# A four-layer MetaFormer block: the first hidden unit and the router of each expert layer fed per image pair, two more casts on GpSimd, routing weights in two fp16 parts

## The reference, cut to what matters

```python
t = t + ffn(_ln_t(t), ...)                     # layer norm over the 64 channels of each pixel
# layer 1 (top 2 logits, softmax over these two); E = 8 experts, H = 256
gate_logits = xf @ Wg + bg
top_w, top_i = top_k(gate_logits, 2); top_w = softmax(top_w)
for e in range(8):
    h = gelu(xf @ W1[e] + b1[e])               # exact gelu
    out = out + w_dense[:, e:e+1] * (h @ W2[e] + b2[e])
# layers 2 and 3: H = 128, probs = softmax(all 8 logits), the two largest are kept as they are
# layer 0: H = 128, one routing per image: logits = mean over pixels @ Wr + br, softmax,
#          scaled by a capacity, softmax again, top 2, softmax; then a second layer norm
```

## Time and profile before

| | |
|---|---|
| median of three runs | 204.16 us |
| the profiled execution's own time | 204.11 us |
| its span, first to last instruction | 202.3 us |
| TensorE busy | 189.9 us (94%) |
| ScalarE / VectorE / GpSimd busy | 124.9 / 122.9 / 42.6 us |
| share of TensorE in the chain that ended last | 75%, VectorE 12%, ScalarE 5% |
| gelu on 128x1024 (L770), 40 of them | 44.4 us |
| down matmuls (L413) | 41.4 us |
| matmuls on zeros (L295), 99 of them | 27.0 us |

### The profile page before, as it was taken

How to read it: one execution, slowest core, us unless ns; L and a number is a source line. 1 busy time by engine, 2 the same in 40 slices (tenths; PEclk the granted TensorE clock), 3 DMA queues, 4 the chain that set the end, 5 groups by cost and what they waited for, 6 DMA issues and landing times.

```text
span 202.3 us, 3039 instructions
## 1 busy us (share of the span) xinstructions
PE 189.9 (94%) x1105; PEld 90.4 (45%) x1113; DVE 122.9 (61%) x342; ACT 124.9 (62%) x206; POOL 42.6 (21%) x60
## 2 busy tenths in 40 slices
PE   7999799889999999899999999999999998699994
PEld 2564222246977866423222346533225496242321
DVE  1358678995750543682824534487575688668565
ACT  2443888646245571876577570497786684588773
POOL 7851100000000000200995000020750022020570
DMA  6999500000000000000000000000000000000001
GB/s 206 369 410 404 209 3 2 0 0 3 0 5 0 0 0 3 0 3 2 0 0 0 0 3 0 0 0 0 0 5 2 0 0 5 0 0 0 0 3 52
DMA packets 3087, 8.54 MB, mean 42 GB/s; under 512 B 520, under 2 KB 1040, under 8 KB 2944
## 3 DMA queue, kind: packets, MB, share of 16 engines
q1 hardware_dynamic: 2736, 7.73, 10.1%
q0 software_dynamic: 192, 0.48, 0.7%
q10 hardware_dynamic: 144, 0.13, 0.3%
HBM read 8.08 MB, written 0.26 MB: 41 GB/s over the span
## 4 chain that ended last, share of the span: by engine, by line
PE 75%; DVE 12%; ACT 5%; issue 3%; POOL 2%; POOLq 1%; DVEq 0%; ACTq 0%
PE bank L413 16%; PE banks L364 8%; PE banks L295 7%; PE banks L365 6%; PE banks L590 6%; PE bank L306 4%; PE banks L348 4%; PE bank L300 3%; POOL total L1452 2%; PE banks L538 2%; PE bank L375 2%; PE bank L660 2%; PE bank L520 2%; ACT hidden L770 2%; PE banks L551 1%
## 5 line engine op out<-in xcount | busy, mean ns | idle before, releaser
L770 ACT ACTIVATE hidden<-banks,pack_l 128x1024 f32<-128x1024 f32 x40 | 44.4, 1113 | 17.0 <-PE banks L365 16.9
L413 PE MATMUL bank<-hidden,w 128*64 128x512 f32 (+1 forms) x160 | 41.4, 596 | 1.5 <-ACT hidden L770 1.5
L295 PE MATMUL banks<-idle_work 128*128 128x512 bf16 x99 | 27.0, 407 | 2.0 <-DVE idle_work L1053 1.2
L364 PE MATMUL banks<-split_x,w_hi 128*128 128x512 f16 x64 | 24.6, 384 | 0.0
L365 PE MATMUL banks<-split_x,w_lo 128*128 128x512 f16 x64 | 24.3, 379 | 0.0
L1443 POOL CAST split_x<-normed 64x256 f16<-64x256 f32 x8 | 3.9, 494 | 96.2 <-DVE normed L935 91.9
L733 ACT ACTIVATE squares<-bank 128x256 f32<-128x256 f32 x18 | 6.9, 383 | 24.1 <-PE bank L300 22.8
L1452 POOL TENSOR_TENSOR total<-total,term 128x512 f32<-128x512 f32 x12 | 17.1, 1424 | 1.9 <-DVE term L1030 1.3
L295 PEld LDWEIGHTS banks<-idle_work 128*128 128x128 bf16 x106 | 10.4, 103 | 14.5 <-issue 4.8
L364 PEld LDWEIGHTS banks<-split_x,w_hi 128*128 128x128 f16 x64 | 6.2, 97 | 23.2 <-issue 14.2
L413 PEld LDWEIGHTS bank<-hidden,w 128*64 128x64 f32 x160 | 7.9, 134 | 18.8 <-issue 16.5
(11 more groups left out here) (310 smaller groups left out, 322.6 us busy)
## 6 DMA issues: line engine op xcount, KB each, us to landing
w_stage<-in_w SPq DMA_DIRECT2D x3, 512.0 KB, 13.6
w_stage<-in_w SPq DMA_DIRECT2D x1, 1024.0 KB, 9.6
conv<-in_conv SPq DMA_DIRECT2D x1, 800.0 KB, 8.1
w<-in_w SPq DMA_DIRECT2D x3, 256.0 KB, 13.8
w<-in_w SPq DMA_DIRECT2D x1, 512.0 KB, 10.4
toeplitz<-in_toeplitz SPq DMA_DIRECT2D x1, 512.0 KB, 11.2
gauss<-in_gauss SPq DMA_DIRECT2D x1, 512.0 KB, 12.7
pack_l<-in_pack_l SPq DMA_DIRECT2D x1, 469.0 KB, 11.9
```

Of the source, the lines that this page charges most:

```text
L295: mm(out, idle_work[:, 0:128], idle_work[:, 0:cols], start=True, stop=True)
L364: mm(out, w1_hi[l][:, at:at + 128], split_x[h][:, :], start=True, stop=False)
L413: last = mm(out[64 * h:64 * h + 64, cut], w2[l][:, (f * NE + e) * CH:(f * NE + e + 1) * CH], hidden[v % 3][:, h * 512 + cut.start:h * 512 ...
L770: act(hidden[u % 3][:, :], both[u % 2][:, :], ACT.Gelu, bias=P(f"l{l}", "e_b1")[:, e * fc + f:e * fc + f + 1]).then_inc(S["moe_gelu"], 1)
```

## The change

It touches four things.

1. **TensorE's order at the start of an expert stage.** `up_straight` takes one chunk at a time (256 columns rather than 512) and waits only for that chunk of `normed`. In layers 1 to 3 the router does tiles 0 and 1 behind the first chunk and tiles 2 and 3 behind the second. In layer 1 the first chunk of unit 1 is also ahead of the second chunk of unit 0. `NORM_TAIL` falls from 4 to 2, 0, 1 and 1 ahead of the four expert stages.
2. **Casts.** ScalarE rounds only chunk 0 of half 0. GpSimd does three: chunk 0 of half 1, chunk 1 of half 1, chunk 1 of half 0. VectorE's last remainder waits for GpSimd's third cast.
3. **Smaller orders.** In layer 1 ScalarE finishes chunk 0's norm ahead of chunk 1's. In layer 0 VectorE takes over the scaling of the router weights, makes the remainders of chunk 0 ahead of the logits, and ScalarE's first exponential stands behind gelu(0).
4. **Routing weights.** The weight is multiplied by 1024 in the step that makes it; one cast writes its fp16 rounding to two places, one subtraction writes the remainder to two places; `select` holds 1/1024. `parts` and `rows` are 128 wide instead of 112, `spread` contracts 32 rows instead of 48.

```diff
-        parts = sb("parts", [128, TILES * 112], BF16)
-        rows = sb("rows", [112, COLS], BF16)
+        parts = sb("parts", [128, TILES * 128], F16)
+        rows = sb("rows", [128, COLS], F16)
...
-        NORM_TAIL = [5, 4, 4, 4, 4, 4, 4, 4, 4]
+        NORM_TAIL = [5, 2, 4, 4, 0, 4, 1, 4, 1]
...
-                    pe.wait_ge(S[f"l{l}_loaded"], 16)
-                    for i in range(TILES):
+                    pe.wait_ge(S["ln_rstd"], 2 * k + 2)
+                    for i in tiles:
                         last = mm(bank[7][:, i * 16:(i + 1) * 16], tile(normed[k], i), P(f"l{l}", "router"),
                                   start=True, stop=True)
-                    last.then_inc(S["route_logits"], 1)
+                    if i == TILES - 1:
+                        last.then_inc(S["route_logits"], 1)
...
-                        pe.wait_ge(S["ln_out"], 2 * k + 2)
+                        pe.wait_ge(S["ln_out"], 2 * k + j + 1)
                     for h in range(HALVES):
                         r = slice(64 * h, 64 * h + 64)
-                        last = mm(both[u % 2][:, h * 512:(h + 1) * 512], stage[l][r, at:at + 128], normed[k][r, :],
-                                  start=True, stop=True)
-                    last.then_inc(S["moe_hidden"], 1)
+                        last = mm(both[u % 2][:, h * 512 + j * PIX:h * 512 + (j + 1) * PIX], stage[l][r, at:at + 128],
+                                  chunk(normed[k], j)[r, :], start=True, stop=True)
+                    if j == INNER - 1:
+                        last.then_inc(S["moe_hidden"], 1)
...
                 for u in range(units):
-                    (up_straight if u < STRAIGHT else up_split)(u)
-                    if u == 0:
-                        router()
-                    if u == 1:
+                    if u == 0 and l == 0:
+                        up_straight(0, 0)
+                        up_straight(0, 1)
+                        router(())
+                    elif u == 0:
+                        up_straight(0, 0)
+                        router((0, 1))
+                        if l == 1:
+                            up_straight(1, 0)
+                        up_straight(0, 1)
+                        router((2, 3))
+                    elif u == 1:
+                        if l != 1:
+                            up_straight(1, 0)
+                        up_straight(1, 1)
                         pe.wait_ge(S[f"w2_loaded{l}"], 16)
+                    else:
+                        up_split(u)
...
-                for j in range(INNER):
-                    sc.wait_ge(S["ln_out"], 2 * k + j + 1)
-                    act(chunk(split_x[0], j)[0:64, :], chunk(normed[k], j)[0:64, :], ACT.Copy)\
-                        .then_inc(S["split_hi0"], 1)
+                sc.wait_ge(S["ln_out"], 2 * k + 1)
+                act(chunk(split_x[0], 0)[0:64, :], chunk(normed[k], 0)[0:64, :], ACT.Copy).then_inc(S["split_act"], 1)
                 nc.scalar.preload_act_table_set("gelu_and_others")
...
-                st.link(TT(g8(rt["weight"][:, :]), g8(rt["picked"][:, :]), spread_to(rs_["inv"][:, :], 8), ALU.mult))
...
-                st.link(V.tensor_copy(part[0], g28("weight")))
-                st.link(TT(g28("rem"), g28("weight"), part[0], ALU.subtract))
-                st.link(V.tensor_copy(part[1], g28("rem")))
-                st.link(TT(part[2], g28("rem"), part[1], ALU.subtract))
-                V.tensor_copy(by_tile[:, :, 64:112], by_tile[:, :, 0:48]).then_inc(S["route_parts"], 1)
+                st.link(STT(g8(rt["weight"][:, :]), g8(rt["picked"][:, :]), PART_SCALE, spread_to(rs_["inv"][:, :], 8),
+                            ALU.mult, ALU.mult))
+                by_part = parts[:, :].rearrange("p (i d a g) -> p i d a g", d=2, a=4, g=16)
+                twice = rt["weight"][:, :].rearrange("p (i g) -> p i g", i=TILES).unsqueeze(2)\
+                    .broadcast_to([128, TILES, 2, 16])
+                st.link(V.tensor_copy(by_part[:, :, :, 0, :], twice))
+                TT(by_part[:, :, :, 1, :], twice, by_part[:, :, :, 0, :], ALU.subtract).then_inc(S["route_parts"], 1)
...
             def split(k, l):
 
-                for j in range(INNER):
+                for j, h in ((0, 1), (1, 1), (1, 0)):
                     po.wait_ge(S["ln_out"], 2 * k + j + 1)
-                    G.tensor_copy(chunk(split_x[1], j)[64:128, :], chunk(normed[k], j)[64:128, :])\
-                        .then_inc(S["split_hi1"], 1)
+                    r = slice(64 * h, 64 * h + 64)
+                    G.tensor_copy(chunk(split_x[h], j)[r, :], chunk(normed[k], j)[r, :]).then_inc(S["split_pool"], 1)
```

69 lines of the change are left out of this document (35 added, 34 removed).

## The result

The changed kernel took 200.97 us (median of four runs, 200.23 to 201.95), the kernel before 203.96 beside it (four runs, 203.74 to 204.27): a ratio of 0.986 [0.983, 0.989]. The forecast was 201.05. The profiled execution took 200.32 us, 3.8 less than the one before, and 1.27 of that fell before the changed code begins.

A forecast was written before the change was run, and what follows sets the result against it. Expert stages were taken as bound by TensorE, their starts by its first real product, layer 0 by VectorE's routing chain. Terms 1.20 + 0.76 + 0.40 + 0.70 = 3.06; 204.11 - 3.06 = 201.05 us, range 200.5 to 202.6.

The forecast's parts named there:

- the forecast's own signs: Whole kernel: wrong if stages gain under 2.4 us, a hole above 0.2 opens ahead of a transpose, or clock under 1.
- Less 0.04 for the extra switches: Layer 3's expert start: deduction from a gain of 0.74 us, leaving 0.70.
- less 0.03: Layer 2's expert start: deduction for switches from a gain of 0.43 us, leaving 0.40.
- I take half of 1.06, 0.53: Up-products at expert starts: a half-width pair costs 0.53 us, so up(0), router, up(1) stay at 3.11 in layer 3.
- The rival: Up-products: a 256-column pair costs 0.64; layers 1 to 3 lose about 0.25, 0.45, 0.45; total 202.2 us; chance 0.12.
- Layer 1: Expert start: down(0) at about 85.36 instead of 86.12, ScalarE late next; gain 0.76 us (0.5 to 0.85).
- Layer 0: Routing chain on VectorE: `rt_less` at 23.36 instead of 24.59; gain 1.20 us (1.0 to 1.25).
- whatever TensorE does: Layer 0: the stage gains what VectorE's routing chain gains, regardless of TensorE; gain 1.20 us.
- in time: Layer 0, ScalarE: the exponential, now behind gelu(0), runs 22.75 to 22.98, before `rt_less` needs it at 23.36.
- Casts and remainders take turns: GpSimd and VectorE exclude each other; TensorE waits 0.5 in layer 3, 0.25 in layer 2; total 202.0 us; chance 0.10.
- The routing parts: Routing tail, layers 1 to 3: 0.6 us less, worth nothing by itself, lets layer 3's 0.70 pass; slack 0.36.
- The clock: TensorE: removing 12 matmuls on zeros ahead of expert stages lets its clock fall; total 209.0 us; chance 0.04.

The follow-up runs named there:

- experiment 1: The changed kernel run again with no edit: 201.72 us median of 10 runs, ratio 0.990.
- regroup: Changed kernel with the router's four tiles together again, behind the second chunk, in the expert stages of layers 1 to 3: 200.72 us, ratio 0.985.
- Experiment 5: Kernel before the change, with only units 0 and 1 going up in two 256-column pieces, still waiting for both chunks: 203.23 us in one run.
- casts_back: Changed kernel with ScalarE again rounding both chunks of half 0, GpSimd two, VectorE's last two remainders swapped: 202.27 us, ratio 0.997.
- exp_first: Changed kernel with layer 0's first exponential again ahead of gelu(0) on ScalarE: 201.92 us in one run.
- experiment 9: Changed kernel with four matmuls on zeros again ahead of every expert stage: 202.17 us in one run.
- no_zeros: Changed kernel without any matmul on zeros but the first 11: 207.26 us, ratio 1.012 without the slowest run.

## Why the prediction was right, and where it was not

**The total.** Within 0.1 of the forecast by luck. The terms summed to 3.06, the change is worth 2.52: 0.54 too much. From the start that the forecast was counted from, that makes 204.11 - 2.52 = 201.59, and experiment 1's run with such a start took 201.68. The profiled execution of after had the fast start, 1.27 in favour, and the median of 200.97 mixes both; with ten runs it is 201.72, and both lie in the range of 200.5 to 202.6. The start's variation, up to 1.3, was not in the range's working, though it is larger than most of the uncertainties that were. By the forecast's own signs, 2.52 passes (2.4 was asked), and no hole opened ahead of a transpose; the third, a granted clock under 1, did come in one of the four runs.

**The price of the pieces (layers 2 and 3): the step that failed.** "Less 0.04 for the extra switches" in layer 3 and "less 0.03" in layer 2 are the mis-sized terms: two more changes between up-products and router products cost 0.30 in each. Behind them stands "I take half of 1.06, 0.53": the 1.06 holds a fixed 0.20 for the group, which does not halve. A half-width pair costs 0.43, near the 0.45 of the earlier trace rows, and 0.63 where it is a group by itself; 0.53 is right only for two in a row. Without the two changes (regroup) layer 2 gains 0.50 and layer 3 0.76. The terms without their deductions were 0.43 and 0.74, and part 4's own 0.05 and 0.03 account for most of the rest: the working of the start holds. The rival had the price of a lone pair (0.64), but charged it to all four pairs and to their width, 0.45 in place of 0.30. Experiment 5 tells them apart: width is free, and from the first up to down(0) the halved pairs in a row take 3.12 (131.26 to 134.38 and 178.11 to 181.23), as taken. The row that one bound was read from the earlier trace rows has the products of one kind in a row, so it could not show what stands between kinds. The Trainium skill (TensorEngine Tiling (Array Packing), "Key Properties") says that a change of tiling mode drains the engine. Up-products use half of the rows (64*128), router products all (128*128), and the trace agrees that a change costs, about 0.15. Whether it is a drain, or weight loads that no product covers, these runs don't show. That rule spoke against this change and was not weighed.

**Layer 1.** 0.71 against 0.76, and close by luck in part. The forecast had gelu(0) held by its table load, which ends 2.92 behind the start of the second average, and up(0) done before it. The load was faster than that (2.81, 78.76 to 81.57), but up(0)'s last piece was later, and gelu(0) started at 2.99 where 2.97 was forecast. So TensorE's switches cost here too: regroup wins 0.18, to 0.89. Undoing either the zeros (0.85) or the cast (0.43) takes much of it away, as both ends must move together.

**Layer 0.** 1.17 against 1.20, but the sentence that layer 0 gains what VectorE's routing chain gains, "whatever TensorE does", is wrong. The first `rt_less` came 1.03 earlier in its stage than before, not 1.23, yet casts_back has it just as early and loses 0.57, and exp_first loses 1.11 with it unmoved. There is a second way: over ScalarE's table load and gelu(0), TensorE's down(0) and up(2), gelu(2), and behind it the second exponential. In the kernel before this way came last. VectorE waited 0.50 at the second `rt_less`, while the exponential itself needs 0.30 with both hand-offs (25.30, when its input is written in the changed kernel, to 25.60); in casts_back it waited 0.92. In the changed kernel gelu(0) comes 1.29 earlier in the stage, the exponential starts as soon as VectorE has written its input, and the 0.30 is all that is left. So the second `rt_less` gains the 1.03 of VectorE's own chain and 0.2 of shorter waiting. The size came out since the working had gelu(0) 1.2 earlier as well. The order of the first exponential, given a clause as "in time", carries 1.1.

**The casts.** The third cast was in time. "Casts and remainders take turns" is out: alone, four remainders and two casts take 4 x 0.42 and 2 x 0.40, 2.48 one after another; they were done in 1.95. `rt_logit` stands right behind the remainders (177.58, they end at 177.55), 0.13 later than TensorE's logits would allow (done at 177.41, and 0.04 for the hand-off), which the slack of 0.54 at the transposes takes in. The Trainium skill (SBUF — State Buffer, "Who interferes with whom") has the shared port as an exclusive lock; by that it would be 2.48, and here the trace shows a slowing of both, casts 0.40 to 0.60 and remainders by 0.27 in four.

**The routing parts.** Forecast nothing by itself, and 0.3 of waiting in layer 3 without it. Measured 0.17 in layer 3, 0.05 in layer 2 and 0.03 in layer 1 (one run), of which 0.03 in each is the transposes' shorter time, which the forecast did not have. The slack was 0.54 instead of 0.36, since the transposes came 0.25 later than forecast, counted from chunk 0's write, and the parts only 0.07.

**The clock.** Held at 0.04 as a way to be slower, and slower it is not: no stretch of a profiled execution of the changed kernel is under 1.00. But five of its fourteen runs had a mean of 0.990 to 0.992, and none of 35 of the kernel before. With the lower level at half the clock, a mean of 0.991 over 200 us is some 3.6 us there (an estimate). If the two groups of these runs belong to the two starts, they cost 1.2 to 1.7 us. So the rival's mechanism seems to be at work at a small part of the price that it named. Where the clock falls, and whether the removed zeros are why, is not shown: no such run was profiled, and none was made with only the zeros put back but the one of experiment 9 (1.000).

**The undone parts don't add.** 1.17 (casts), 1.10 (exponential), 1.35 (zeros) and 0.24 (parts) are 3.86, more than 2.52. Two of them gate the same gelu(0) in layers 0 or 1, and the gain is there only with both.

**Open.** What sets the moment at which the pace of the first matmuls doubles: it came between about 4 us and beyond 6 us in the profiled executions of all these kernels, whatever had been edited (halves_only, the kernel before plus one edit, had the mixer at 8.62). And the clock of the slower runs, as said above.

## What to carry to other kernels

Work that starts on the first half of its data gains what the wait was, less a fixed price for each change between kinds of product: cut it so that products of one kind stay together, even when one half starts a step later. When two engines hand work back and forth, the one that is busy without gaps is not yet the bound: undo one order on the other engine and look. And read a gain per stage from a fixed event, since a start that varies by 1.3 us can make a wrong sum look right. Look at the granted clock of every run too, and not only at that of the profiled one.

## What the runs showed of the hardware

- A change between products over 64 rows and over 128 rows, both fp32, cost about 0.15 us: 0.20 for each group of up-products beside 0.43 a half-width pair, 0.10 for each group of router products. Splitting 512 columns into twice 256 cost nothing (1.06 both ways).
- The eleven first matmuls took 3.94 to 4.88 us between executions. They ran at 0.43 us apart and then at 0.22, by a step at about 4 us in one trace and behind all eleven in another, while the recorded granted clock reads 1.00 in both. In the traces with the late step the first of the mean's products (256 columns of fp32) took 634 ns and later ones 379, and 634 is also what products of this form took at a recorded grant of 0.50 (no_zeros). So the first matmuls seem to run at the lower level without the record showing it.
- GpSimd's casts and VectorE's subtractions with two inputs slowed each other but did not exclude each other: a cast took 0.60 in place of 0.40, and four subtractions 1.95 in place of 1.68.
- VectorE's small scaling took 0.23 once and 0.46 the second time in layer 0, 16 columns wide in both cases. The second stood wholly beside GpSimd's casts, the first for its last 0.14 only. Three traces have the same two durations; that the casts are the cause was not tested.
- With the zeros left out, the grant of 0.50 began half a microsecond behind the idle stretch and held through 4 us of dense work; so a filler can save more than the idle time that it covers.
